# A selective scan with PE's sum of two products moved inside the step, and a loop body twice as long

## The reference

```
dA = exp(delta_t * A)                    # per channel and state
h  = h * dA + (delta_t * u_t) * B_t      # recurrence over t
y_t = sum over the 16 states of h * C_t
```

## Time and profile before

| what | us |
|---|---|
| median of 3 runs | 35231.98 (35160.76 to 35288.79) |
| the profiled execution's own time | 35258.12 |
| its span, first to last instruction | 35256.3 |
| mean granted clock of TensorE, share of full speed | 0.777 |
| PE matmul busy | 26406.9 (75%) |
| DVE busy | 24871.2 (71%) |
| POOL busy | 21995.5 (62%) |
| ACT busy | 15127.5 (43%) |

### The profile page before, as it was taken

One profiled execution on the slowest core, in us unless ns is written; L12 is line 12 of the kernel. 1 busy time (PEld: TensorE's weight loads), 2 busy tenths in 40 slices (PEclk: granted clock), 3 DMA queues, 4 the chain that ended last, 5 costly groups with the idle time before them and its releaser, 6 DMA issues. The chain is left out here.

```text
span 35256.3 us, 353348 instructions
## 1 busy us (share of the span) xinstructions
PE 26406.9 (75%) x100774; PEld 8372.0 (24%) x100774; DVE 24871.2 (71%) x15541; ACT 15127.5 (43%) x20404; POOL 21995.5 (62%) x9902
## 2 busy tenths in 40 slices
PE   7857888885547788888876668888873758888884
PEld 3422222221223322222223222222211322222221
DVE  1237999997322289999981269999983139999995
ACT  1044555553233345555511345555541245555551
POOL 0016999996000089999930149999980029999991
PEclk8857888887667778888867668888876768888887
DMA  1022122213212222221243221222124232122214
GB/s 67 10 116 77 40 48 47 48 42 102 80 67 96 97 52 48 48 47 40 47 151 122 105 87 43 44 47 45 42 61 159 94 110 44 43 47 48 47 42 147
DMA packets 928980, 2422.06 MB, mean 69 GB/s; under 512 B 113744, under 2 KB 331668, under 8 KB 919504
## 3 DMA queue, kind: packets, MB, share of 16 engines
q1 hardware_dynamic: 927000, 2398.76, 24.4%
HBM read 1375.34 MB, written 1023.05 MB: 68 GB/s over the span
## 5 line engine op out<-in xcount | busy, mean ns | idle before, releaser
L1086 POOL TENSOR_TENSOR scan_hc<-scan_bc,scan_h 128x1024 f32<-128x1024 f32 x6912 | 16089.6, 2352 | 716.1 <-DVE scan_h L1248 712.5
L1248 DVE TENSOR_TENSOR_SCAN scan_h<-scan_da,scan_state,scan_dbu 128x1024 f32<-128x1024 f32 x6912 | 15983.3, 2335 | 246.4 <-ACT scan_da L1138 237.8
L1169 PE MATMUL scan_da<-scan_dd,scan_ssel 32*128 32x512 f32 x27648 | 9456.1, 776 | 2807.7 <-DVE scan_h L1248 2610.9
L1138 ACT ACTIVATE scan_da<-scan_da,scan_a_cur 128x1024 f32<-128x1024 f32 x6912 | 7517.9, 1088 | 8291.5 <-PE scan_da L1169 8286.9
L1169 PE MATMUL scan_p_du<-scan_dd,scan_ssel 32*128 32x512 f32 x27648 | 9670.6, 781 | 657.9 <-DMA scan_bc<-bc_d 197.7
L1235 DVE TENSOR_TENSOR scan_dbu<-scan_p_du,scan_bc 128x1024 f32<-128x1024 f32 x4608 | 5553.9, 1205 | 1008.8 <-PE scan_p_du L1169 986.4
L1072 POOL TENSOR_TENSOR scan_dbu<-scan_bc,scan_dus 128x1024 f32<-128x1024 f32 x2304 | 5420.9, 2353 | 154.5 <-ACT scan_dus L1112 148.4
L1169 PEld LDWEIGHTS scan_da<-scan_dd,scan_ssel 32*128 32x128 f32 x27648 | 2562.4, 224 | 10345.9 <-DVE scan_h L1248 8310.3
L1186 PE MATMUL scan_p_y<-scan_hc,scan_rsel 128*32 128x512 f32 x27648 | 4930.3, 795 | 6.7 <-POOL scan_hc L1086 6.7
L1169 PEld LDWEIGHTS scan_p_du<-scan_dd,scan_ssel 32*128 32x128 f32 x27648 | 2491.8, 219 | 3817.4 <-DVE scan_dbu L1235 2937.0
L856 PE MATMUL prep_p_dt<-prep_dtv,prep_wdt 12*128 12x384 f32 x2304 | 1449.3, 789 | 1930.7 <-DVE prep_delta L914 1730.8
(11 more groups left out here) (202 smaller groups left out, 13865.8 us busy)
## 6 DMA issues: line engine op xcount, KB each, us to landing
scan_bc<-bc_d SPq DMA_DIRECT2D x576, 512.0 KB, 12.3
du_d<-prep_du SPq DMA_DIRECT2D x384, 576.0 KB, 2.8
delta_d<-prep_delta SPq DMA_DIRECT2D x384, 576.0 KB, 3.7
scan_dd<-delta_d SPq DMA_DIRECT2D x1152, 192.0 KB, 4.8
scan_dd<-du_d SPq DMA_DIRECT2D x1152, 192.0 KB, 6.6
y_d<-scan_y SPq DMA_DIRECT2D x576, 384.0 KB, 5.1
merge_y<-y_d SPq DMA_DIRECT2D x384, 576.0 KB, 3.8
xs_d<-proj_xs_o SPq DMA_DIRECT2D x96, 588.0 KB, 3.4
```

What stands on the lines that cost most here:

```text
L1086: nc.gpsimd.tensor_tensor(hc[:, u % HC_SLOTS, :], c, h[:, u % H_SLOTS, :], ALU.mult).then_inc(hc_ready, 1)
L1138: nc.scalar.activation(da[u % DELTA_BANKS][:], da[u % DELTA_BANKS][:], ACT.Exp, scale=a_cur[:, u // UNITS, u % UNITS:u % UNITS + 1]).then_ ...
L1169: return nc.tensor.matmul(dst[:, half * H:(half + 1) * H], ssel[rows, i, :], dd[rows, s, m, j, :], start=True, stop=True)
L1248: nc.vector.tensor_tensor_scan(h[:, v % H_SLOTS, :], da[v % DELTA_BANKS][:], dbu[:, v % DBU_SLOTS, :], state[:, v % UNITS:v % UNITS + 1], ...
```

## The change

1. `SUM_LAG` goes from 8 to 9, and in PE's step the call of `reduce` moves: it stood behind P(u) and ahead of D(u) at even u; it now stands behind D(u) at odd u. The pair summed in step u is then (u-9, u-8).
2. `UNROLL` goes from 2 to 4, so a round has 192 units and there are 9 rounds in place of 18. A new constant `CHUNK_SLOTS` = 2 keeps the buffers `dd`, `bc`, `a_cur` and the semaphores `loaded` at two slots; indices that were u // 48 now go through `slot(u)`. SP's loop runs over `CHUNK_SLOTS` and keeps its 17 turns, in the same order.

```diff
-UNROLL = 2
+UNROLL = 4
+CHUNK_SLOTS = 2
-SUM_LAG = 8
+SUM_LAG = 9
-        dd = ph.sb("dd", [P, UNROLL, TILES, BLOCKS, H])
-        bc = ph.sb("bc", [P, UNROLL, 2 * IMAGES, T])
+        dd = ph.sb("dd", [P, CHUNK_SLOTS, TILES, BLOCKS, H])
+        bc = ph.sb("bc", [P, CHUNK_SLOTS, 2 * IMAGES, T])
...
+        TURNS = UNROLL // CHUNK_SLOTS
         def slot(u):
-            return u // UNITS % UNROLL, u // ROUND
+            c = u // UNITS
+            return c % CHUNK_SLOTS, c // CHUNK_SLOTS + 1
...
                     for u in range(ROUND):
-                        if u % UNITS == UNITS - 1 and not (last and u > UNITS):
+                        if u % UNITS == UNITS - 1 and not (last and u == ROUND - 1):
                             s, n = slot(u + TRIO)
-                            t.wait_ge(loaded[s], r * LOADS + (n + 1) * LOADS + ONE)
+                            t.wait_ge(loaded[s], r * (TURNS * LOADS) + n * LOADS + ONE)
...
                             spread_share(r, u + TRIO)
-                        if u % PAIR == 0 and (u >= SUM_LAG or not first):
-                            reduce(r, u - SUM_LAG)

                         t.wait_ge(scanned, nth(q, u - DELTA_BANKS + 1) + ONE)
                         spread(da[u % DELTA_BANKS], 0, u, 0)
                         spread(da[u % DELTA_BANKS], 0, u, 1).then_inc(delta_spread, 1)
+                        if u % PAIR == 1 and (u >= SUM_LAG or not first):
+
+                            reduce(r, u - SUM_LAG)
...
-                for u in range(ROUND - SUM_LAG, ROUND, PAIR):
+                for u in range(ROUND - SUM_LAG + 1, ROUND, PAIR):
                     reduce(ROUNDS - 1, u)
```

More of the change, by code:

```diff
@@ L987, in scan @@
         carry = ph.sb("carry", [P, ALL_CHUNKS])
-        a_cur = ph.sb("a_cur", [P, UNROLL, UNITS + 1])
+        a_cur = ph.sb("a_cur", [P, CHUNK_SLOTS, UNITS + 1])
         ssel = ph.sb("ssel", [P, PER_QUAD, P])
         rsel = ph.sb("rsel", [P, PER_QUAD, QUAD])
-        dd = ph.sb("dd", [P, UNROLL, TILES, BLOCKS, H])
-        bc = ph.sb("bc", [P, UNROLL, 2 * IMAGES, T])
+        dd = ph.sb("dd", [P, CHUNK_SLOTS, TILES, BLOCKS, H])
+        bc = ph.sb("bc", [P, CHUNK_SLOTS, 2 * IMAGES, T])
         dus = ph.sb("dus", [P, DUS_SLOTS, T])
@@ L1004, in scan @@
         a_ready = ph.sem("a_ready")
-        loaded = [ph.sem(f"loaded{s}") for s in range(UNROLL)]
+        loaded = [ph.sem(f"loaded{s}") for s in range(CHUNK_SLOTS)]
         delta_spread = ph.sem("delta_spread")
@@ L1051, in store @@
                                          y[half * 64:(half + 1) * 64, b::2, :]).then_inc(y_stored, 16)
-                for s in range(UNROLL):
+                for s in range(CHUNK_SLOTS):
                     load(s * T, s)
[L1055 to L1061, removed]
+                with sp.Fori(0, (ALL_CHUNKS - CHUNK_SLOTS) // CHUNK_SLOTS) as i:
+                    for s in range(CHUNK_SLOTS):
+                        store(i * CHUNK_SLOTS + s, i * (CHUNK_SLOTS * T) + s * T)
+                        load(i * (CHUNK_SLOTS * T) + (s + CHUNK_SLOTS) * T, s)
+                for s in range(CHUNK_SLOTS):
+                    store(ALL_CHUNKS - CHUNK_SLOTS + s, (ALL_CHUNKS - CHUNK_SLOTS + s) * T)
                 sp.wait_ge(y_stored, STORES * ALL_CHUNKS + ONE)
@@ L1070, in share @@
                     g.sem_inc(passed, 1)
-                    s = u // UNITS % UNROLL
+                    s, _ = slot(u % ROUND)
                     nc.gpsimd.tensor_tensor(dbu[:, u % DBU_SLOTS, :], bc[:, s, image(u % UNITS), :],
@@ L1084, in rounds @@
                             g.wait_ge(reduced, nth(r * (ROUND // PAIR), (u - HC_SLOTS) // PAIR + 1) + ONE)
-                        c = bc[:, u // UNITS, IMAGES + image(u % UNITS), :]
+                        c = bc[:, slot(u)[0], IMAGES + image(u % UNITS), :]
                         nc.gpsimd.tensor_tensor(hc[:, u % HC_SLOTS, :], c, h[:, u % H_SLOTS, :],
@@ L1114, in keep @@
                 def keep(r, u):
-                    v, s = u % ROUND, u // UNITS % UNROLL
+                    v, s = u % ROUND, u // UNITS % CHUNK_SLOTS
                     a.wait_ge(scanned, r * ROUND + (u + 1) + ONE)
@@ L1138, in rounds @@
                         nc.scalar.activation(da[u % DELTA_BANKS][:], da[u % DELTA_BANKS][:], ACT.Exp,
-                                             scale=a_cur[:, u // UNITS, u % UNITS:u % UNITS + 1]).then_inc(da_ready, 1)
+                                             scale=a_cur[:, slot(u)[0], u % UNITS:u % UNITS + 1]).then_inc(da_ready, 1)
                         if u % EIGHT == 0 and (u >= 2 * EIGHT or not first):
                             evacuate(r, u // EIGHT - 2)
-                        if u % UNITS == UNITS // 2 and not (last and u > UNITS):
+                        if u % UNITS == UNITS // 2 and not (last and u > ROUND - UNITS):
                             chunk = r * UNROLL + (u // UNITS + 1)
-                            constants_of(chunk, (u // UNITS + 1) % UNROLL)
+                            constants_of(chunk, (u // UNITS + 1) % CHUNK_SLOTS)
                 a.wait_ge(consts, 64 + ONE)
@@ L1166, in spread @@
                 def spread(dst, n, u, half):
-                    s, (m, j, i) = u // UNITS % UNROLL, unit(u % UNITS)
+                    s, (m, j, i) = u // UNITS % CHUNK_SLOTS, unit(u % UNITS)
                     rows = slice((2 * n + half) * QUAD, (2 * n + half + 1) * QUAD)
@@ L1229, in times_b @@
                     if u % UNITS == 0:
-                        d.wait_ge(loaded[u // UNITS], r * LOADS + LOADS + ONE)
+                        s, n = slot(u)
+                        d.wait_ge(loaded[s], r * (TURNS * LOADS) + n * LOADS + ONE)
                     d.wait_ge(du_spread, r * (ROUND // TRIO * 2) + (u // TRIO * 2 + u % TRIO + 1) + ONE)
                     d.wait_ge(scanned, nth(r * ROUND, u - DBU_SLOTS + 1) + ONE)
-                    nc.vector.tensor_tensor(dbu[:, u % DBU_SLOTS, :], p_du[:], bc[:, u // UNITS, image(u % UNITS), :],
+                    nc.vector.tensor_tensor(dbu[:, u % DBU_SLOTS, :], p_du[:], bc[:, slot(u)[0], image(u % UNITS), :],
                                             ALU.mult).then_inc(dbu_ready, 1)
```

## The result

| | before | changed |
|---|---|---|
| median, us | 35206.53 (4 runs) | 41549.94 (4 runs, 41544.60 to 41555.08) |
| ratio | 1 | 1.180, 95% interval 1.1775 to 1.1822 |
| profiled execution, us | 35258.12 | 41555.08 |
| granted clock, whole span | 0.777 | 0.665 |

The change makes the kernel 18% slower. The prediction was 41350 us.

The account below looks back on a forecast made before the run. POOL and DVE both near their floors in the scans, PE's clock behind them. 35258 (profiled) + 6220 (Q behind D) - 100 (joints) = 41378, less 26 to the median: 41350 us; range 37600 to 43300.

Parts of the forecast that it names:

- The order at DVE and PE: In the scans, Q starts only after D at odd steps and the next P stands behind it, so DVE waits.
- Q between D(5) and P(6): On PE, the new order parts D(5) and P(6), which overlapped; T(6) 1.21 us late (high clock), 3.90 (low).
- T(3) and T(6): DVE's operations to be late above all: 0.09 and 1.21 us at the high clock, 3.68 and 3.90 at the low.
- The high-clock term: A six-unit period followed with PE at its high clock: 19.34 us in the new order.
- POOL's 18.5: POOL's floor for a six-unit period, in us; the old order's period at the high clock.
- The clock: In the scans, thinner PE records lower the clock: low level 0.76 of the time, period 24.5 us, +6220 us.
- my mixture of the two periods: Scan period taken as 19.34 us plus the low-clock share times 6.80, up to 26.14 us when always low.
- Records per us: PE's records in the scans: fewer go with the low clock; forecast some 75 to 80 in 26 us.
- B of the chances: Rival: the scans' clock stays high throughout, about 35410 us; chance 0.05.
- rival C: Faster: PE runs P ahead of a ready Q, so POOL's floor rules the scans; 34500 to 34900 us; chance 0.07.
- The joints: 36 fewer joints between loop rounds, 0 to 3.9 us saved each, 0 to 140 in all; taken as -100 us.
- H needs no slot: POOL's H needing a summed pair's slot starts after Q ends: 12.57 against 11.27 us, low clock 16.16 against 14.48.

Follow-up runs that it names:

- e3: The changed kernel with Q still at odd steps and SUM_LAG 9, but ahead of D; 34626 us, ratio 0.983.
- e7: The changed kernel with the Q of step 5 moved one step later and ahead of D, the other two left behind D; 36171 us, ratio 1.026.
- e11: The changed kernel with eight zero-weight records added ahead of D at three of four even steps; 39865 us, ratio 1.132.
- e4: The changed kernel with every Q run twice, the second time with zero weights (24 more records per six units); 43530 us, ratio 1.235.
- e10: The changed kernel with zero-weight records added at Q, half as many as in e4 (12 per six units); 43348 us, ratio 1.230.
- e1: The changed kernel with rounds of two chunks in place of four, Q behind D at odd steps; 41532 us, ratio 1.178.
- e2: The kernel before with rounds of four chunks in place of two, Q left at even steps ahead of D; 35048 us, ratio 0.995.
- e13: e3 with rounds of two chunks in place of four (Q at odd steps, ahead of D); 34849 us, ratio 0.990.
- e6: e2 with zero-weight records added at Q, half as many as in e5; 34781 us, ratio 0.987.
- e5: e2 with every Q run twice, the second time with zero weights; 34816 us, ratio 0.988.

## Why the prediction was right, step by step

**The order at DVE and PE: right.** "Q between D(5) and P(6)" is what e3 and e7 take away, and the loss goes with it, all of it in e3 and most of it in e7. The two T that were to be late, T(3) and T(6), are the 2301 waits; T(4), by hand 0.52 us late at the low clock and not at the high one, waited in five of 1152 periods. That a Q stands alone is in the trace of the kernel before: no record of a D or a P starts between its eight, and its first starts 517 ns behind the last one of P (median of 3440), where from a D's record to a P's next to it the median is 7 ns. By hand a period lost 8.1 us at the low clock and 1.3 at the high one; 6.47 was measured.

**The high-clock term: right.** 19.34 by hand, 19.24 in e11. Against POOL's 18.5 that is 0.74 us x 1152 = 850 us, 14% of the 6298. That the other 86% are the clock's doing is this subtraction and the rows at both levels; no run held the clock high throughout in the new order.

**The clock: right in direction and, with luck, in size.** I took 0.76 of the time at the low level and 24.5 us. The scan clock of 0.65 is a share of (1 - 0.65) / 0.5 = 0.70, and the period 24.56. Two errors met: my share was 0.06 too high, worth 0.06 x 6.80 x 1152 = 470 us, and with the measured share my mixture of the two periods gives 19.34 + 0.70 x 6.80 = 24.10 us, 0.46 x 1152 = 530 us too little. The mixture was loose from the start: the prediction's 18.5 and about 22.7 us for the old order, with a third of the time low, make 19.9 us, and the kernel before ran at 19.10. It would hold if the low clock fell anywhere; in the changed kernel it lies within the stretch of D(5), Q and P(6) in 1147 of 1148 periods, so that T(6) waits 3.81 us, nearly the 3.90 of the low level, while T(3) waits 2.68 of 3.68. Mixed with their measured shares, e4 comes to 21.5 + 0.44 x 10.5 = 26.1 us and measured 26.3; e10 comes to 20.4 + 0.44 x 8.6 = 24.2 and measured 26.1.

**Records per us: right here, no rule.** 15156 x 26 / 5180 = 76 records in 26 us, forecast 75 to 80. But from run to run they don't settle the clock: e10 has 84 at 0.78, the kernel before 98 at 0.83, and e11 has 101 at 0.75. So the prediction's step from thin stretches to a low clock holds between stretches of one kernel, and the number of records alone doesn't decide it. What the prediction set against a clock that is always low, that it rises behind stretches in which PE has been working without a break, is in the traces: in the scans of the kernel before 1396 of 1403 rises come behind 3.0 us or more of PE without a gap and none of 1402 falls does, with 26% of the time lying so far behind a gap; in the changed kernel it is 1193 of 1608 rises and none of 1605 falls. What else decides it no run shows. That the slower loop lowers the clock and the lower clock slows the loop was argued; no run separates the two directions.

**A clock that stays high throughout, B of the chances (35258 + 276 - 100 - 26, about 35410 us, where 276 is 1152 x (19.34 - 19.10)), is out.** In the first scan of the changed kernel PE is, by the profile, matmul-busy for 5763 of 7076 us, only one of its gaps is longer than 1.5 us (2.34 us), and the clock is low for 70% of the time. In each of 3436 stretches of one Q the record ahead of it is a D's and the next one behind it a P's, the program's order, which is why rival C (faster, PE taking P first) fell. C was right in one thing: POOL's floor was to be had, and e3 reaches it, 5335 us for the first scan, 18.5 us a period, by leaving Q ahead of D.

**The joints: wrong in bounds, too small to matter.** I had 0 to 3.9 us for a joint saved and took -100 us. In the new order it is nothing (e1 against the changed kernel: 18 us the other way), the lower bound. In the old order 36 joints fewer gave 159 us (e2; 127 to 215 by its interval) and 223 us (e13 to e3), 4.4 and 6.2 us each. The second is clearly above my upper bound of 3.9, the first only by its middle. The likely reason is that I had counted the wait at the joint and not the small waits of the units behind it, which DVE has while it has no lead over POOL. Why PE stands still at a joint no run shows; there are the 2.84 us of "issue" in the earlier trace rows and the time saved.

**"H needs no slot": half right.** H did wait for Q at its slot, 1950 us in 1148 waits, once a period, although I had it covered. It cost nothing: DVE has not one wait for POOL in the changed kernel, so the period is DVE's and PE's. In e3 and e7, where Q is less late, it is 0 and 197 us.

## What to carry to other kernels

On an engine that works in program order, as PE does in these traces (D, Q, P around each of the 3436 Q), an operation that nobody waits for soon belongs ahead of the operation that has to wait anyway, not behind it: there it pushes the one that somebody does wait for (34626 us in e3 with Q ahead of D, 41550 with it behind). Follow one period by hand at each clock level: this order costs the period 4% at the high clock (19.24 against 18.5 us), and 29% as it ran (24.56 against 19.10). And look at which operations the low clock covers, and what it makes of work that you add: a better mean clock came with a slower kernel when the added work stood on the path (e4).

## What was not expected of the hardware

- With zero-weight matmuls added the granted clock was higher: 0.84 to 0.95 with 12 records added to 72 per period (e6), and 24 do no more (e5).
- The clock locks onto the pattern. In the changed kernel the low clock lies within the stretch of D(5), Q and P(6) in 1147 of 1148 periods, all 1605 falls within the scans come behind the D of an even step, which has no Q behind it, and 1142 periods take 24 to 26 us; in the kernel before they spread from under 18 to 25.
- A joint of the loop costs 4.4 to 6.2 us of the kernel's time where DVE and POOL are both near their floors, and nothing that shows where PE is late anyway.
- Not settled: why the clock still falls in e11 with filling at three of four even steps. Of 918 falls in its scans 746 (81%) come behind the D of the even step that has no filling (u mod 8 = 0) or the next one. So those steps are the likely cause; filling them too was not tried.
